# Three 32-head attentions: query products that share terms go on adding in their PSUM bank between reads

## What is computed

```python
# l1x: queries from x, keys and values from a context, a bias for each head
q = (h @ Wq).reshape(16, 64, 32, 128);  scores = q @ k.T / sqrt(128) + bias
# l3a: 32 query heads, 8 key heads; queries and keys are rotated (rope)
q = q * cos + rotate_half(q) * sin;     scores = causal(q @ k.T / sqrt(128))
# l3x: 32 query heads, 8 key heads; queries and keys are divided by their root mean square (rms)
q = q * rsqrt(mean(q * q) + 1e-6) * w;  scores = q @ k.T / sqrt(128)
x = x + softmax(scores) @ v @ Wo        # all three
```

## Time and profile before

| | us |
|---|---|
| median of 3 runs | 4101.63 |
| lowest and highest | 4099.48, 4105.89 |
| span of the profiled execution | 4096.2 |
| PE busy, share of the span | 3831.2, 94% |
| DVE busy | 2440.9, 60% |
| ACT busy | 1407.5, 34% |
| POOL busy | 550.2, 13% |
| l1x, from its first query product to its last output product | about 1341 to 1890 |
| l3a, from its first key product on | about 2628 to 3283 |
| l3x, from its first key product on | about 3294 to 4043 |

### The profile page before, as it was taken

The page is one execution under the profiler, slowest core; times in us unless marked ns, Lnnn a source line. Parts: engine busy times, 40 slices in busy tenths (PEclk is TensorE's granted clock), DMA queues, the critical chain, the costliest instruction groups (busy, mean ns, idle before and its releaser), DMA issues. The chain is left out here.

```text
span 4096.2 us, 49760 instructions
## 1 busy us (share of the span) xinstructions
PE 3831.2 (94%) x18570; PEld 2050.3 (50%) x18570; DVE 2440.9 (60%) x4102; ACT 1407.5 (34%) x2522; POOL 550.2 (13%) x520
## 2 busy tenths in 40 slices
PE   8899989998988899999999889789999989999997
PEld 3343435554455455554447664345455555555564
DVE  0988955552246545444448658876766665555563
ACT  2988935552233211111113334211111133333332
POOL 1111111220001211100000111121211111000000
PEclk9999999999999999999999989999999999999998
DMA  5111111001100433311000022100001021111110
GB/s 190 54 37 52 56 67 34 32 29 65 39 34 14 181 114 113 124 47 75 1 31 39 1 104 59 66 8 34 21 21 42 1 69 37 37 37 36 42 37 24
DMA packets 133960, 215.31 MB, mean 53 GB/s; under 512 B 42576, under 2 KB 95057, under 8 KB 123105
## 3 DMA queue, kind: packets, MB, share of 16 engines
q1 hardware_dynamic: 133728, 212.19, 14.8%
HBM read 168.12 MB, written 44.04 MB: 52 GB/s over the span
## 5 line engine op out<-in xcount | busy, mean ns | idle before, releaser
L559 PE MATMUL l1x_po<-l1x_wo,l1x_cT 128*128 128x512 f32 x512 | 230.9, 596 | 1.2 <-issue 1.2
L1206 PE MATMUL l3a_po<-l3a_wo,l3a_cT 128*128 128x512 f32 x512 | 229.5, 596 | 1.2 <-ACT l3a_cT L1403 1.2
L1206 PEld LDWEIGHTS l3a_po<-l3a_wo,l3a_cT 128*128 128x128 f32 x512 | 95.6, 190 | 119.9 <-issue 115.5
L559 PEld LDWEIGHTS l1x_po<-l1x_wo,l1x_cT 128*128 128x128 f32 x512 | 96.5, 191 | 116.8 <-issue 116.7
L1094 PE MATMUL l3a_pj<-kvT,l3a_ws 128*128 128x512 f32 x256 | 121.4, 608 | 11.9 <-POOL l3a_ws L998 10.3
L1094 PE MATMUL l3x_pj<-kvT,l3x_ws 128*128 128x512 f32 x256 | 120.4, 602 | 0.1
L1206 PE MATMUL l3x_po<-l3x_wo,l3x_cT 128*128 128x512 f32 x256 | 115.3, 593 | 0.7 <-ACT l3x_cT L1403 0.7
L1206 PE MATMUL l3x_pc<-l3x_wo,l3x_cT 128*128 128x512 f32 x256 | 115.2, 592 | 0.0
L2235 DVE TENSOR_SCALAR_CACHE_REDUCE l0a_keep<-l0a_keep,l0a_scalars 128x1376 uint16<-128x1376 uint16 x64 | 105.4, 1646 | 3.6 <-DVE l0a_scalars L2241 1.5
L2682 POOL TENSOR_TENSOR l0x_q<-l0x_q,l0x_qi 128x512 f32<-128x512 f32 x64 | 65.4, 1044 | 303.6 <-DVE l0x_qi L2970 303.6
L3129 PE MATMUL l1f_ph<-l1f_w,l1f_xT 128*128 128x448 f32 x256 | 104.7, 558 | 0.0
(11 more groups left out here) (575 smaller groups left out, 8485.1 us busy)
## 6 DMA issues: line engine op xcount, KB each, us to landing
l1x_kb<-l1x_keys SPq DMA_DIRECT2D x32, 512.0 KB, 4.7
l1x_vb<-l1x_values SPq DMA_DIRECT2D x32, 512.0 KB, 3.4
l1x_keys<-l0a_kv SPq DMA_DIRECT2D x40, 256.0 KB, 2.0
fill_wk<-in_L_xattn_Wk SPq DMA_DIRECT2D x8, 1024.0 KB, 5.8
kvT<-in_L_xattn_Wv SPq DMA_DIRECT2D x8, 1024.0 KB, 5.6
l1x_values<-l0a_kv SPq DMA_DIRECT2D x32, 256.0 KB, 2.3
l1x_wq<-in_L_xattn_Wq SPq DMA_DIRECT2D x8, 1024.0 KB, 6.5
l1x_sbias<-in_L_xattn_bias SPq DMA_DIRECT2D x8, 1024.0 KB, 7.4
```

The costliest lines, as they stand in the source:

```text
L559: mm = pe.matmul(po[:, t % 2, :], cT[:, u, h, t * P:(t + 1) * P], wo[:, u, h, :], start=h == 0, stop=h == GH - 1)
L1206: mm = pe.matmul(outs[t % 2][:, :], cT[:, h, t * P:(t + 1) * P], wo[:, u, h, :], start=h == 0, stop=h == GH - 1)
```

## The change

- P3 is added by PE to P1 in its bank, P5 to P1+P3, and P6 to P4: these three steps no longer start their bank (`more_of_bank`). The bank is read between them: ACT copies P1, then P1+P3, then P1+P3+P5 (`saved` 1, 3, 5). DVE adds a kept block to P2, to P4, to P4+P6 and to P7 (`summed` 2, 4, 6, 7), and each of its four results is one of the four query blocks.
- The joins go: three sums for each pair, on DVE in l1x and l3x, on POOL in l3a. There are two kept blocks instead of three.
- DVE's sum with P3 goes, and one with P4 comes. In DVE's order it stands where the joins stood or behind `shift`: at the border of groups in l3a and l3x the order is now `scaled`, `shift`, sum with P4, sum with P6.
- P5 waits for ACT's copy of P1+P3, and P6 for DVE's sum with P4, since these read the bank that the step adds to. P6 waited for ACT's copy of P4 before (in l1x and l3x), or for the same and stood ahead of P5 (in l3a).
- In l3a and l3x all steps run in the order 1 to 7. P6 of the next group stands behind `turns` of head 2, not ahead of it, and P7 of pair 0 ahead of P1 of pair 1, not behind it.
- P3 waits for the second sum of weight blocks only, P5 for the third and P6 for the fourth. `mix` of the other pair starts after P6 (in l3a it started after P5, behind the joins).

The diff, cut to its core (`stage_gqa`; `stage_bias` is changed in the same way, without the moves on PE):

```diff
@@ POOL
-                def join(n, p):
-                    ...
-                    nc.gpsimd.tensor_tensor(keep(1), keep(0), keep(1), ALU.add).then_inc(q_joined, 1)
-                    ...
-                    nc.gpsimd.tensor_tensor(keep(0), keep(0), keep(2), ALU.add).then_inc(q_joined, 1)
-                    ...
-                    nc.gpsimd.tensor_tensor(query(1, 1), keep(1), keep(2), ALU.add).then_inc(q_joined, 1)
@@ PE
                     elif k == 3:
-                        pe.wait_ge(mixed, mixed_at(n, p, 3) + 2)
+                        pe.wait_ge(mixed, mixed_at(n, p, 1) + 2)
                         pe.wait_ge(q_saved, saved_at(n, p, 1) + 2)
                     elif k == 4:
                         pe.wait_ge(q_summed, summed_at(n, p, 2) + 2)
                     elif k == 5:
-                        pe.wait_ge(q_summed, summed_at(n, p, 3) + 2)
+                        pe.wait_ge(mixed, mixed_at(n, p, 2) + 2)
+                        pe.wait_ge(q_saved, saved_at(n, p, 3) + 2)
                     elif k == 6:
-                        pe.wait_ge(q_saved, saved_at(n, p, 4) + 2)
+                        pe.wait_ge(mixed, mixed_at(n, p, 3) + 2)
+                        pe.wait_ge(q_summed, summed_at(n, p, 4) + 2)
...
-                        mm = pe.matmul(pj[:, p if k % 2 else 1 - p, :], weights, stream, start=c == 0, stop=c == 1)
+                        more_of_bank = k in (3, 5, 6)
+                        mm = pe.matmul(pj[:, p if k % 2 else 1 - p, :], weights, stream, start=c == 0 and not more_of_bank,
+                                       stop=c == 1, skip_group_check=more_of_bank)
...
                 def group(n, u, behind, more):
+                    step(n, u, 0, 7)
                     if behind:
                         step(n, u, 1, 1)
-                    step(n, u, 0, 7)
...
                     scores(n, u, 3)
                     if more:
-                        step(n + 1, 1 - u, 0, order[4])
-                        step(n + 1, 1 - u, 0, order[5])
+                        step(n + 1, 1 - u, 0, 5)
...
                     turns(n, 2)
+                    if more:
+                        step(n + 1, 1 - u, 0, 6)
@@ DVE
                         summed(n + 1, 0, 2)
                         rotate(n + 1, 0, 0)
-                        summed(n + 1, 0, 3)
                     scaled(n, 3)
+                    shift(3)
                     if more:
-                        join(n + 1, 0)
-                    if rope:
-                        shift(3)
-                    if more:
+                        summed(n + 1, 0, 4)
                         summed(n + 1, 0, 6)
-                    if rms:
-                        shift(3)
-                    if more:
-                        join_both(n + 1, 0)
                         rotate(n + 1, 0, 1)
```

More of the change, by code:

```diff
@@ L1218, in opening @@
                     all_keys(0, 0)
-                    for k in order[1:6]:
+                    for k in range(2, 7):
                         step(0, 0, 0, k)
@@ L1250, in group @@
                     scores(n, u, 1)
-                    step(n, u, 1, order[4])
+                    step(n, u, 1, 5)
                     if behind:
@@ L1254, in group @@
                         attend(n - 1, 2)
-                    step(n, u, 1, order[5])
+                    step(n, u, 1, 6)
                     if behind:
@@ L1276, in group @@
                         all_keys(n + 1, 1 - u)
-                        for k in order[1:4]:
+                        for k in (2, 3, 4):
                             step(n + 1, 1 - u, 0, k)
@@ L1285, in group @@
                     turns(n, 2)
-                    if not more:
+                    if more:
+                        step(n + 1, 1 - u, 0, 6)
+                    else:
                         out(n - 1, 1 - u, 7)
@@ L1548, in rotate @@
+                    if rope and pair(n, p):
+                        dve.wait_ge(rotated, turn_q(n if p else n - 1, h + (0 if p else 2), j) + 2)
+                    nc.vector.tensor_tensor(query(h, j), keep(h), pj[:, p if k % 2 else 1 - p, :],
+                                            ALU.add).then_inc(q_summed, 1)
                 def rotate(n, h, j):
                     if rope:
-                        if h % 2 and j:
-                            dve.wait_ge(q_joined, joined_at(n, h // 2, "both") + 2)
-                        else:
-                            dve.wait_ge(q_summed, summed_at(n, h // 2, {(0, 0): 2, (0, 1): 6, (1, 0): 7}[h % 2, j]) + 2)
+                        dve.wait_ge(q_summed, summed_at(n, h // 2, {(0, 0): 2, (1, 1): 4, (0, 1): 6, (1, 0): 7}[h % 2, j]) + 2)
@@ L1666, in group @@
                     scaled(n, 0)
-                    if behind:
-                        summed(n, 1, 3)
                     shift(0)
```

152 lines of the change are left out of this document (44 added, 108 removed).

## The result

| | before | after |
|---|---|---|
| median of the runs, both measured side by side, us | 4103.41 (4099.48 to 4105.89) | 4127.75 (4124.6 to 4132.25) |
| ratio, 95% interval | | 1.006 (1.0048 to 1.0072) |
| span of the profiled execution | 4096.2 | 4123.0 |

What follows compares the result with a forecast made beforehand. The prediction took PE's work as the bound. Seven l3a groups at 1.65 + 0.4 and seven l3x borders at 1.1 gave 22.1 us, so 4101.6 + 22.1 = 4123.7 us, with a range of 4104 to 4142.

Steps and rivals of the forecast that it cites:

- PE bounds, relief of DVE and POOL is worth nothing: All stages: PE's work sets the time, so about 66 us less work on DVE gains nothing.
- The l3a border, 1.65: Each of seven group borders in l3a gets 1.65 us longer, although the 1.47 us wait for POOL goes; bounds 0.4 and 2.6.
- P6's wait: At group borders PE waits for DVE's sum with P4 before P6: 1.15 us in l3a, 1.85 in l3x.
- the rotation: l3a border: under POOL's mix DVE's rotation of query(0,1) is stretched by 1.24 us, products 2.23 for 1.40, sum 1.10 for 0.69.
- the wait of scores: l3a border: PE waits 1.5 us for the rotation before scores of head 0.
- Mid group of l3a, 0.4: P6 of pair 1 waits 0.4 us for DVE's sum with P4, in each of seven groups; bounds 0 and 0.7.
- The l3x border, 1.1: Each of seven group borders in l3x gets 1.1 us longer; bounds 0.6 and 1.7.
- l1x, 0: In l1x transposes and an output product cover P6's wait for DVE's sum with P4: 0 us.
- Openings and first groups, 0 each, bounds 2: First group of each of three stages: 0 us, bounds -2 and +2; spared DVE work stands against waits on P6.
- Full exclusion of POOL and DVE: Rival, chance 0.07: three rotation operations each wait for a whole POOL instruction, l3a borders 0.95 us longer each, 4130 us.
- A clock that falls at the borders: Rival, chance 0.11: PE's waits lower its clock at seven borders, 1.7 us each, 12 more, 4136 us.
- The wait is hidden: Rival, chance 0.09: DVE's sum with P4 is done in time at l3a and l3x borders, old waits go, 4088.6 us.
- Given back: Rival, chance 0.11: relieved DVE comes earlier to the rest of the group, returning the border's loss, about 4102 us.

Runs made afterwards that it cites:

- mid_sum: Changed kernel, with DVE's sum with P4 put ahead of the add of output block 2 in mid group of l3a: 4128.31 us, ratio to before 1.0061.
- l1x_only: Kernel before, with the change made in l1x alone: 4104.37 us, ratio to before 1.0000.
- p5_ahead: Changed kernel, with P5 ahead of head 3's scores and DVE's sum with P4 ahead of `scaled` at l3a borders: 4124.63 us, ratio to before 1.0051.
- l3a_only: Kernel before, with the change made in l3a alone: 4127.87 us, ratio to before 1.0059.
- sum4_ahead: Changed kernel, with DVE's sum with P4 ahead of `shift` of head 3 at l3x borders: 4122.67 us, ratio to before 1.0052.
- mix_late: Changed kernel, with POOL's mix for pair 1 in l3a started after P1 of pair 1 instead of P6: 4129.26 us, ratio to before 1.0062.

## Why the prediction was right

The mechanism was right at each place that it named: the same waits came, in the same order. The size of the whole agrees better than its parts do. The steady groups were forecast 22.1 us longer and are 25.0 longer in the trace, a fall of the clock of 1.5 included; that the medians differ by 24.3 is partly luck, since they scatter by some 4 us. Of the 4.05 us by which the forecast missed 4127.75, 1.8 is the median of before, 4103.41 with one more run and 4101.63 in the forecast.

- **PE bounds, relief of DVE and POOL is worth nothing.** Right: 91 and 77 us less work, and in the steady groups PE's waits are most of what moved: in l3a the three new waits of a border and the one in mid group, less the old 1.47, are 1.92 of the 2.24 that a period grew.
- **The l3a border, 1.65.** From the start of P5 to that of P3 it took 12.47 before (P6 and P5 in the other order) and 14.37 after: 1.90. The terms of it, forecast and measured: P6's wait 1.15 and 1.11; the rotation 2.2 and 1.1 long, 2.23 and 1.10; the wait of scores 1.5 and 1.56; the wait for `weighed` 0.5 and 0.32. The 0.25 that I missed lies in small things: P6 started 3.53 after P5, not 3.37 (the step took 1.82 and not 1.77, and PE started 0.14 after the end of the sum), and the steps behind it took 1.8 each.
- **Mid group of l3a, 0.4.** Measured 0.40 in the row, and 0.45 by `mid_sum`. The period of l3a grew by 2.24 for a forecast of 2.05, and the seven borders by 17.1 for 14.4. The difference is 7 x 0.19 and the one fall of the clock, 1.5.
- **The l3x border, 1.1.** P6's wait 1.75 for 1.85; the period grew by 1.1, the seven borders by 7.9 for 7.7.
- **l1x, 0**: +0.8 us in the profile, nothing by `l1x_only`. **Openings and first groups, 0 each, bounds 2**: -0.8 in l3a and +1.0 in l3x. The tail of l3x, of which I had said nothing, was 2.4 longer, with 13.7 us at the lower clock where before had 6.8. The code of l3x doesn't fix this: `mid_sum` and `p5_ahead` have the same l3x code as after, and there it was 6.8 again and the tail as short as before. But the 13.7 came in no profile with the old l3x code (of four), and in four of the eight with the new one. So whether the change makes it likelier is open.

**The rivals.** *Full exclusion of POOL and DVE* would have made the rotation 0.95 longer at each border. It took what rows 4 and 6 had shown. From 2954.79 to 2958.88 DVE did four instructions that take 2.8 us alone, and POOL three that take 2.2 alone, nearly all of them inside that time: 5.0 us of work in 4.1. They hinder each other, by some 0.42 us for each instruction but the first on either engine, but don't take turns as wholes. Whether they take turns for a part of each instruction, these rows don't tell. The Trainium skill (SBUF — State Buffer, section "Who interferes with whom") calls the port pair that both use an exclusive lock; in its section "SBUF: two separate sides" the page says that whichever instruction starts first has the pair for the whole instruction and the other is blocked. This trace doesn't agree: 0.42 and not 0.73. *A clock that falls at the borders* is the rival that happened, but once of seven times. In after it fell right behind the waits of the fifth border of l3a; stretches with columns as in rows 1:

```profile
3038.00:3040.00 2.00, 0.80 (x2) 0.00 (x0) 1.97 (x2) 0.00 (x0) 1.67 (x2) 1.00 0.00 0
3040.00:3042.00 2.00, 1.32 (x33) 1.21 (x34) 1.93 (x5) 0.00 (x0) 0.00 (x0) 1.00 0.00 0
3042.00:3044.00 2.00, 2.00 (x6) 1.19 (x6) 1.94 (x4) 1.07 (x2) 0.00 (x0) 0.52 0.00 0
3044.00:3046.00 2.00, 2.00 (x4) 0.86 (x3) 1.14 (x3) 0.00 (x0) 0.00 (x0) 0.62 0.04 8
3046.00:3050.00 4.00, 4.00 (x15) 1.75 (x14) 3.90 (x6) 1.27 (x3) 0.00 (x0) 1.00 0.00 0
```

The granted clock went to its lower level for some 3 us, and P2 took 3.21 from start to start instead of 1.82. That period was 82.85 instead of 81.35, which is 1.5, close to the 1.7 that I had put for a fall. The other six borders, with the same idle times of PE, kept 1.00. The other profiles say a little more. The five kernels that keep the wait of 1.56 for the rotation (after, `l3a_only`, `mid_sum`, `sum4_ahead`, `p5_ahead`) had 5 falls at their 35 borders of l3a, each for 1.4 to 1.6 us. The other seven had none at 49: 21 of these have before's single wait of 1.47, and 14 the wait of 1.11 without the one of 1.56. So a fall seems to need the wait of 1.56 and what stands around it; that is a count, and not an experiment. *The wait is hidden* fell with the first row: P6 waited at each border. *Given back* fell with the periods: nothing of the 2.2 came back in the 79 us behind it.

## What to carry to other kernels

When the bounding engine is 98% busy, ask of each edit only where that engine waits and who ends the wait; the work that other engines are spared is worth nothing, and a value that is now read out of a bank between two steps puts its reader's whole queue between them. So place the reader ahead of all work that isn't due (in l3x one line of DVE's order was worth 1 us a group). See too whether it waits for yet another engine: in l3a it did, for ACT's copy, and P5 had to move on PE as well. And look at what a third engine runs beside the reader at that time. And before a scheme is rebuilt for the sake of one wait, loosen that wait alone: three semaphore waits gave 9 us, where the rebuilt scheme lost 24 and, repaired at four places, came out even.

## What was not expected of the hardware

- Adding up in a bank that ACT or DVE had read in between cost PE nothing that shows: at the full clock a step of four matmuls in l3a took 1.72 to 1.91 us from start to start in before, and 1.72 to 1.82 in after.
- What POOL's sum hinders depends on the instruction. In `mix_late` DVE's reduction with one input (L1532) took 0.68 under POOL's sum, the same as alone, and POOL's sum its 0.72. The product with two inputs (L1536) that followed took 1.11. The Trainium skill (SBUF — State Buffer, section "Who interferes with whom") has this division too: a DVE instruction with at most one input in SBUF, outside its 2-port modes, does not contend with GpSimd. The trace agrees.

```profile
2966.38 0.72 POOL L965 TENSOR_TENSOR l3a_ws<-l3a_wq 128x256 f32<-128x256 f32 x1 [22.69 <-PE l3a_pj L1054]
2966.39 0.68 DVE L1532 TENSOR_REDUCE l3a_tot<-l3a_sc 128x8 f32<-128x512 f32 x1
```

- The same instructions with the same idle times kept the full clock at one border and lost it at another, and unchanged stretches differed by up to 9 us between executions. For terms of 1 us the period in the trace is the measure, and the median is not.
